# Another order of one turn's pieces on four engines of a two-layer transformer kernel

## The chip, the core and the metric

The kernel runs on one core of a Trainium2 chip. PE is the matrix engine (TensorE), ACT the scalar engine, DVE the vector engine, POOL is GpSimd, SP issues the DMAs. The engines run beside each other and meet through semaphores. The metric is the device time of one execution in microseconds (us).

## The reference, cut to what matters

The input has 32 sequences of 256 tokens with 128 features, all in fp32. Four sublayers follow one another, each with a residual and a layer norm behind it.

```
x = layernorm(x + mala_attn(x))      # a: rotary linear attention, 8 heads, 5-tap conv on v, gate
x = layernorm(x + low_rank_moe(x))   # b: base matmul + one of four low-rank experts (top-1 softmax)
x = layernorm(x + causal_attn(x))    # c: softmax attention in 256 tokens
x = layernorm(x + routed_swiglu(x))  # r, d: grouped top-4 of 16 experts, plus two shared ones
#   g = silu(x @ w1.T); u = x @ w3.T; y = sum_e comb[e] * (g * u)[e] @ w2[e].T + shared
```

## The kernel before, in words

The tokens are cut into 16 blocks of 512 tokens (four tiles of 128). A block goes through five stages, one per turn: **a** (first attention), **b** (low-rank layer and the projections of the second attention), **c** (second attention, and the router **r**), **d** (the experts), **e** (last residual and store). Turn i works on block i in stage a, i-1 in b, i-2 in c, i-3 in d and i-4 in e, so there are 20 turns; in turns 4 to 15 all five stages are there. Six turns are written out ahead (LEAD), ten run in a hardware loop of two turns per pass, and four are written out behind.

Each engine has its own function `turn`, a list of calls in the order in which the engine does them. Nothing is reordered by a scheduler: an engine waits at the first call whose semaphores are not there. The order written in `turn` is therefore the whole plan.

The experts are 9 chunks of 128 hidden units (8 routed, 1 shared). For a chunk c:
- PE `d_hidden(n, odd, c)`: gate part into bank GB and up part into UB. Each is three fp32r matmuls of 512 columns (`mm3`, L331 to L333: high*high, high*low, low*high). For c from 1 to 7 it ends with `d_spread` (L542, a bf16 matmul that spreads the routing weights over 512 columns into CB).
- ACT `d_silu` (L729): silu of GB. DVE `d_gu` (L1041): times UB. DVE `d_hid` (L1051): times CB. Chunk 8 has no routing weight and goes through L1044.
- PE `d_down(n, c)` (L552): the fp32 matmul with w2, accumulated in YB. One such matmul is two records in the trace. `d_down(n, 8)` is the last; ACT `d_y` (L733) copies YB behind it.

GB, UB and CB exist once. So `d_hidden(c+1)` waits for `d_silu(c)` and `d_gu(c)`, and `d_spread(c)` waits for `d_hid(c-1)`.

Pieces of the other stages stand between the chunks. Those the text speaks of, in the order of their data:
- b: `b_small` (PE L443) -> `b_norm`, `b_logits` (DVE L877 to L895, POOL L1183 between) -> `b_exp` (ACT L681) -> `b_first`, `b_weigh` (DVE L900 to L924, the last writes `down_x`) -> `b_dnT` (PE L340 of down_x) -> ACT copy L689 -> `b_up` (PE L455/L456) -> `b_res` and its statistics (DVE L982, L859) -> `ln_of(1)` (POOL L1163, ends with `shift`) -> `b_layer_norm` (ACT L643) -> `c_xT` (PE L340 of x2) -> `c_project`, `c_value` (PE L466, L467, L472).
- r: `r_xT`, ACT `r_hi` (L714, L715), `r_gate` (PE L512), ACT `r_exp` (L719), DVE `r_groups` and `r_combine` (L1006 to L1035, the last writes `comb`), POOL `r_split` (L1138 to L1144), PE `d_cT` of the next turn.
- POOL also has `x3_lo` (L1202), `x2_bias` (L1192), `e_norm` (L1212, L1216) and `c_norm` (L1206, L1208).
- a: `a_kv`, `a_qT_`, `a_den`, `a_num_` (PE L396, L340, L413, L418), `a_rd`, `a_out` (L428); on DVE four `conv_tap` (L933).
- c: `c_pT` (PE L493), ACT L710, `c_av` (PE L499 to L501).

Exp and silu need different function tables on ACT; an ACT_TABLE_LOAD stands where the kind changes.

## Time and profile before

| what | value |
|---|---|
| median of 3 runs | 835.02 us (834.77 to 835.66) |
| span of the profiled execution | 831.0 us |
| PE busy | 759.4 us, 91% |
| DVE busy | 607.2 us, 73% |
| ACT busy | 455.8 us, 55% |
| POOL busy | 416.1 us, 50% |

The page gives the profiled execution's span, from first to last instruction, and no separate time for it; the median of the runs is 4.0 us above the span. Matmul records overlap (the end of one is modelled and lies past the start of the next), so for PE the distance from start to start is what a matmul costs, and not the duration printed in its row.

### The profile page before, as it was taken

The page shows a single profiled execution, that of the slowest core. Times are in us where ns is not written, and L with a number is a line of the kernel's source. Part 1 is how long each engine was busy: PE and PEld are TensorE (multiplying, and loading weights), DVE is VectorE, ACT ScalarE, POOL GpSimd, SP SyncE. Part 2 cuts the span into 40 slices and gives each one's busy share as a digit, 9 for nine tenths or more (in the row PEclk, how much of TensorE's full clock was granted, in tenths as well). Part 3 has the DMA queues.
Part 4 walks back from the last instruction along what each step waited for, and adds up shares of the span by engine and source line. Part 5 has one row for each costly group of instructions (what it writes and reads, how often), then busy time and mean ns, then how long its engine had stood idle before and what let it go on. Part 6 is the DMA issues. An engine that isn't in the chain of part 4 may idle for free.

```text
span 831.0 us, 13767 instructions
## 1 busy us (share of the span) xinstructions
PE 759.4 (91%) x3926; PEld 537.0 (65%) x3926; DVE 607.2 (73%) x1853; ACT 455.8 (55%) x863; POOL 416.1 (50%) x922
## 2 busy tenths in 40 slices
PE   4487689999999999999999999999999999999985
PEld 3375667676767676666767676667767676665552
DVE  2554748878797878778797878788796878785652
ACT  2224266575656666664655666664656666655321
POOL 2425534664646545654636555654636555543322
PEclk9658789999999999999999999999999999999998
DMA  5000000000000000000000000000000000000000
GB/s 222 13 0 14 0 14 1 14 14 13 2 13 14 14 14 13 14 13 13 0 13 13 13 13 13 14 13 13 0 13 13 13 0 13 2 13 0 13 13 13
DMA packets 17526, 13.04 MB, mean 16 GB/s; under 512 B 576, under 2 KB 16960, under 8 KB 17088
## 3 DMA queue, kind: packets, MB, share of 16 engines
q1 hardware_dynamic: 17472, 12.47, 4.7%
q14 instruction: 38, 0.31, 0.1%
q8 instruction: 16, 0.26, 0.1%
HBM read 8.27 MB, written 4.19 MB: 15 GB/s over the span
## 4 chain that ended last, share of the span: by engine, by line
PE 68%; DVE 12%; issue 9%; ACT 5%; POOL 4%; DMA 1%; DVEq 0%; POOLq 0%; SPq 0%; ACTq 0%
PE bank L552 12%; PE bank L340 7%; PE bank L331 6%; PE bank L333 6%; PE bank L332 6%; PE bank L542 4%; PE bank L455 2%; PE bank L428 2%; PE bank L472 2%; PE bank L443 2%; PE bank L413 2%; PE bank L466 2%; PE bank L467 2%; PE bank L371 2%; DVE hid L1051 2%
## 5 line engine op out<-in xcount | busy, mean ns | idle before, releaser
L1041 DVE TENSOR_TENSOR gu<-silu,bank 128x512 f32<-128x512 f32 x128 | 86.5, 676 | 108.3 <-ACT silu L729 72.8
L552 PE MATMUL bank<-hid,whole 128*128 128x512 f32 x288 | 152.9, 614 | 0.3 <-DVE hid L1044 0.3
L331 PE MATMUL bank<-x3T_hi,w_hi 128*128 128x512 f32 x288 | 141.2, 490 | 0.1
L729 ACT ACTIVATE silu<-bank 128x512 f32<-128x512 f32 x144 | 85.8, 596 | 86.8 <-PE bank L333 80.5
L333 PE MATMUL bank<-x3T_hi,w_lo 128*128 128x512 f32 x288 | 113.9, 396 | 0.0
L332 PE MATMUL bank<-x3T_lo,w_hi 128*128 128x512 f32 x288 | 113.7, 395 | 0.0
L1051 DVE TENSOR_TENSOR hid<-gu,bank 128x512 f32<-128x512 f32 x128 | 87.3, 682 | 9.4 <-DVE gu L1041 3.4
L1132 POOL TENSOR_TENSOR qk<-rope_c,rope_s 128x512 f32<-128x512 f32 x32 | 40.6, 1280 | 72.2 <-DVE rope_s L830 72.2
L1163 POOL TENSOR_TENSOR moment<-stats 128x4 f32<-128x4 f32 x192 | 35.9, 219 | 79.1 <-DVE stats L859 78.9
L331 PEld LDWEIGHTS bank<-x3T_hi,w_hi 128*128 128x128 f32 x288 | 54.7, 190 | 21.6 <-issue 10.3
L1163 POOL TENSOR_TENSOR rstd<-moment,whole 128x4 f32<-128x4 f32 x64 | 64.8, 1012 | 5.0
L332 PEld LDWEIGHTS bank<-x3T_lo,w_hi 128*128 128x128 f32 x288 | 54.9, 191 | 16.0 <-issue 10.3
L1150 POOL TENSOR_TENSOR rden_x<-rden,whole 128x512 f32<-128x512 f32 x16 | 17.4, 1088 | 93.1 <-DVE rden L843 93.1
L552 PEld LDWEIGHTS bank<-hid,whole 128*128 128x128 f32 x288 | 46.4, 189 | 25.8 <-DVE hid L1044 13.2
L333 PEld LDWEIGHTS bank<-x3T_hi,w_lo 128*128 128x128 f32 x288 | 54.2, 188 | 12.6
L729 ACT ACT_TABLE_LOAD x45 | 57.7, 1283 | 0.8
L859 DVE BATCH_NORM_STATS2 stats<-res 128x6 f32<-128x128 f32 x256 | 55.8, 281 | 2.2
L542 PE MATMUL bank<-combT,sel_exp_b 48*128 48x512 bf16 x128 | 49.7, 388 | 5.5 <-DVE hid L1051 4.8
L933 DVE SCALAR_TENSOR_TENSOR conv<-vT,whole,conv 128x512 f32<-128x512 f32 x64 | 48.1, 751 | 0.3
L542 PEld LDWEIGHTS bank<-combT,sel_exp_b 48*128 48x128 bf16 x128 | 11.8, 92 | 49.6 <-issue 30.6
L340 PE MATMUL bank<-whole,x 128*128 128x128 f32 x192 | 31.2, 287 | 11.7 <-ACT x L643 8.2
L676 ACT ACTIVATE numT<-bank,v_sum 128x256 f32<-128x256 f32 x32 | 13.4, 470 | 51.8 <-PE bank L418 51.8
(210 smaller groups left out, 1850.7 us busy)
## 6 DMA issues: line engine op xcount, KB each, us to landing
x_in<-x SPq DMA_DIRECT2D x16, 256.0 KB, 3.1
out<-x SPq DMA_DIRECT2D x16, 256.0 KB, 2.3
whole<-w_whole SPq DMA_DIRECT2D x1, 1198.5 KB, 5.6
w_raw<-w SPq DMA_DIRECT2D x1, 1152.0 KB, 9.3
whole<-w_whole SPq DMA_DIRECT2D x1, 1088.0 KB, 11.3
w_raw<-w SPq DMA_DIRECT2D x1, 546.0 KB, 6.9
```

Of the source, the lines that this page charges most:

```text
L331: mm(out, wh, mh, start=True, stop=False)
L332: mm(out, wh, ml, start=False, stop=False)
L333: return mm(out, wl, mh, start=False, stop=True)
L340: last = nc.tensor.transpose(out[0:parts, t * P:(t + 1) * P], src(t), eye)
L542: mm(CB[:], sel_exp_b[:, c * P:(c + 1) * P], combT[:], start=True, stop=True).then_inc(p_C.sem, 1)
L552: mm(YB[:], whole[:, a:a + P], hid[:, c % 2], start=c == 0, stop=c == CHUNKS).then_inc(p_w2.sem, 1)
L729: fn(silu[:, c % 2], GB[:], ACT.Silu).then_inc(a_silu.sem, 1)
L859: nc.vector.bn_stats(stats[k][:, t, :], res[k][:, t, :]).then_inc(v_st[k].sem, 1)
L933: stt(conv[:], vT[:, :, j:j + SEQ], taps[:, j:j + 1], conv[:], ALU.mult, ALU.add).then_inc(v_conv.sem, 1)
L1041: tt(gu[:, c % 2], silu[:, c % 2], UB[:], ALU.mult).then_inc(v_gu.sem, 1)
L1051: tt(hid[:, c % 2], gu[:, c % 2], CB[:], ALU.mult).then_inc(v_hid.sem, 1)
L1163: tt(out, in0, in1, op).then_inc(g_ln[k].sem, 1)
```

## The change

The same calls are made with the same operands; only their order in the four `turn` functions differs. No matmul, activation or vector operation is added or removed, but two ACT table loads per turn fall away, since the exps of b and r now follow one another.

```diff
@@ -560,47 +560,47 @@
                 if d: d_hidden(i - 3, 1 - odd, 0)
                 if d: d_cT(i - 3, live(i - 1))
                 if c: c_scores(i - 2)
+                if a: a_xT_(i, odd, load)
                 if d: d_spread(i - 3, 0)
-                if a: a_xT_(i, odd, load)
                 if e: d_yT(i - 4)
                 if d: d_hidden(i - 3, 1 - odd, 1)
+                if a: a_v_(i)
                 if d: d_down(i - 3, 0)
-                if a: a_v_(i)
                 if d: d_hidden(i - 3, 1 - odd, 2)
                 if c: c_pT(i - 2)
                 if a: a_qk(i)
-                if d: d_down(i - 3, 1)
                 if c: c_av(i - 2)
                 if b: b_xT(i - 1)
+                if d: d_down(i - 3, 1)
+                if a: a_g_(i)
+                if b: b_small(i - 1)
+                if a: a_vT_(i)
                 if d: d_hidden(i - 3, 1 - odd, 3)
-                if b: b_small(i - 1)
-                if a: a_g_(i)
                 if d: d_down(i - 3, 2)
-                if a: a_vT_(i)
                 if d: d_hidden(i - 3, 1 - odd, 4)
+                if a: a_kv(i)
+                if a: a_qT_(i)
                 if d: d_down(i - 3, 3)
-                if a: a_kv(i)
                 if d: d_hidden(i - 3, 1 - odd, 5)
+                if a: a_den(i)
                 if c: r_xT(i - 2, odd)
-                if a: a_qT_(i)
+                if a: a_num_(i)
                 if d: d_down(i - 3, 4)
                 if c: r_gate(i - 2)
                 if b: b_dnT(i - 1)
                 if d: d_hidden(i - 3, 1 - odd, 6)
-                if a: a_den(i)
                 if b: b_up(i - 1)
-                if a: a_num_(i)
                 if d: d_down(i - 3, 5)
+                if a: a_rd(i)
                 if d: d_hidden(i - 3, 1 - odd, 7)
-                if a: a_rd(i)
                 if d: d_down(i - 3, 6)
                 if d: d_hidden(i - 3, 1 - odd, 8)
                 if d: d_down(i - 3, 7)
-                if d: d_down(i - 3, 8)
                 if b: c_xT(i - 1)
                 if a: a_out(i)
                 if b: c_project(i - 1)
                 if b: c_value(i - 1)
+                if d: d_down(i - 3, 8)
 
             for i in range(LEAD):
                 if i == 3:
@@ -740,18 +740,18 @@
                 if d: d_silu(i - 3, 1)
                 if c: c_exp(i - 2)
                 if a: a_v_(i)
+                if c: c_pT(i - 2)
                 if d: d_silu(i - 3, 2)
-                if c: c_pT(i - 2)
                 if b: copy_xT(i - 1, 1, B0)
+                if b: b_small(i - 1)
                 if d: d_silu(i - 3, 3)
-                if b: b_small(i - 1)
                 if a: a_g_(i)
                 if a: a_vT_(i)
                 if d: d_silu(i - 3, 4)
+                if a: a_qT_(i)
+                if d: d_silu(i - 3, 5)
                 if b: b_exp(i - 1)
-                if d: d_silu(i - 3, 5)
                 if c: r_hi(i - 2, odd)
-                if a: a_qT_(i)
                 if c: r_exp(i - 2)
                 if b: b_dnT(i - 1)
                 if d: d_silu(i - 3, 6)
@@ -760,8 +760,8 @@
                 if d: d_silu(i - 3, 8)
                 if b: b_layer_norm(i - 1)
                 if b: copy_xT(i - 1, 2, B0)
+                if b: c_qkv(i - 1)
                 if d: d_y(i - 3)
-                if b: c_qkv(i - 1)
 
             for i in range(LEAD):
                 if i == 1:
@@ -1066,40 +1066,40 @@
                 if d: d_gu(i - 3, 1)
                 if d: d_hid(i - 3, 1)
                 if b: a_layer_norm(i - 1)
+                if a: a_rope(i)
                 if d: d_gu(i - 3, 2)
+                if c: c_res(i - 2)
                 if d: d_hid(i - 3, 2)
-                if a: a_rope(i)
-                if c: c_res(i - 2)
+                if b: b_norm(i - 1, 0)
                 if d: d_gu(i - 3, 3)
-                if b: b_norm(i - 1, 0)
+                if b: b_norm(i - 1, 1)
                 if d: d_hid(i - 3, 3)
-                if b: b_norm(i - 1, 1)
+                if b: b_logits(i - 1)
                 if d: d_gu(i - 3, 4)
-                if b: b_logits(i - 1)
+                if a: a_kv(i)
                 if d: d_hid(i - 3, 4)
-                if a: a_kv(i)
+                if a: conv_tap(i, 1)
                 if b: b_first(i - 1)
-                if b: b_weigh(i - 1)
-                if a: conv_tap(i, 1)
                 if d: d_gu(i - 3, 5)
                 if a: conv_tap(i, 2)
+                if b: b_weigh(i - 1)
                 if d: d_hid(i - 3, 5)
                 if a: conv_tap(i, 3)
                 if c: r_groups(i - 2, 0)
                 if a: conv_tap(i, 4)
                 if c: r_groups(i - 2, 1)
+                if a: a_den(i)
+                if c: r_groups(i - 2, 2)
                 if d: d_gu(i - 3, 6)
-                if c: r_groups(i - 2, 2)
-                if a: a_den(i)
                 if b: b_res(i - 1)
+                if d: d_hid(i - 3, 6)
                 if c: r_groups(i - 2, 3)
-                if d: d_hid(i - 3, 6)
-                if c: r_groups(i - 2, 4)
+                if a: a_att(i)
                 if d: d_gu(i - 3, 7)
                 if d: d_hid(i - 3, 7)
-                if a: a_att(i)
+                if c: r_groups(i - 2, 4)
+                if a: a_gate(i)
                 if d: d_gu(i - 3, 8)
-                if a: a_gate(i)
                 if c: r_combine(i - 2)
                 if a: a_res(i, odd)
 
@@ -1223,13 +1223,13 @@
                 if c: ln_of(2, i - 2)
                 if b: b_norm(i - 1)
                 if c: c_norm(i - 2, odd)
-                if e: e_norm(i - 4)
-                if c: x3_lo(i - 2, odd)
                 if a: a_rd(i)
                 if b: ln_of(1, i - 1)
                 if a: a_mix(i)
+                if b: x2_bias(i - 1)
+                if c: x3_lo(i - 2, odd)
                 if c: r_split(i - 2)
-                if b: x2_bias(i - 1)
+                if e: e_norm(i - 4)
                 if a: ln_of(0, i)
 
             for i in range(LEAD):
```

How the order stands, word for word. In the names, `whole` is the block of constants (w2 and the identity among them), `x_b` is x2 with its bias, a buffer number is left out.

PE, the end of a turn, before:

```order
L333 MATMUL bank<-x3T_hi,w_lo 128x512
L552 MATMUL bank<-hid,whole 128x512 x2
L340 MATMUL bank<-whole,x 128x128 x4
L428 MATMUL bank<-whole,oT 128x128 x4
L466 MATMUL bank<-x2T,w_raw 128x512
L467 MATMUL bank<-x2T,w_raw 128x512
L472 MATMUL bank<-w_raw,x2T 128x128 x4
```

PE, the same place in the change and the first matmul of the next turn:

```order
L333 MATMUL bank<-x3T_hi,w_lo 128x512
L552 MATMUL bank<-hid,whole 128x512
L340 MATMUL bank<-whole,x 128x128 x4
L428 MATMUL bank<-whole,oT 128x128 x4
L466 MATMUL bank<-x2T,w_raw 128x512
L467 MATMUL bank<-x2T,w_raw 128x512
L472 MATMUL bank<-w_raw,x2T 128x128 x4
L552 MATMUL bank<-hid,whole 128x512
L331 MATMUL bank<-x3T_hi,w_hi 128x512
```

The last down-projection (L552) moved from right behind the one before it to the end of the turn, ahead of the next turn's first chunk.

PE, the middle of a turn from the spread of chunk 5 on, before:

```order
L542 MATMUL bank<-combT,sel_exp_b 128x512
L340 MATMUL bank<-whole,x_1 128x128 x4
L340 MATMUL bank<-whole,qk 128x128 x4
L552 MATMUL bank<-hid,whole 128x512
L512 MATMUL bank<-w_raw,x3T 128x16 x4
L340 MATMUL bank<-whole,down_x 96x128 x4
L331 MATMUL bank<-x3T_hi,w_hi 128x512
```

The same place in the change:

```order
L542 MATMUL bank<-combT,sel_exp_b 128x512
L413 MATMUL bank<-ks_m,qT 128x8 x4
L340 MATMUL bank<-whole,x_1 128x128 x4
L418 MATMUL bank<-qT,kv_m 128x256 x2
L552 MATMUL bank<-hid,whole 128x512
L512 MATMUL bank<-w_raw,x3T 128x16 x4
L340 MATMUL bank<-whole,down_x 96x128 x4
L331 MATMUL bank<-x3T_hi,w_hi 128x512
```

`a_den` and `a_num_` (L413, L418) stand ahead of the router's matmul (L512) and of `down_x`; before, they came a chunk later, on both sides of `b_up`.

ACT, the middle of a turn, before:

```order
L729 ACTIVATE silu<-bank 128x512
L681 ACT_TABLE_LOAD
L681 ACTIVATE lg_e<-lg_s 128x16
L729 ACT_TABLE_LOAD
L729 ACTIVATE silu<-bank 128x512
L714 ACTIVATE x3T<-bank 128x512
L715 ACTIVATE x3T_hi<-bank 128x512
L661 ACTIVATE qT<-bank 128x512
L719 ACT_TABLE_LOAD
L719 ACTIVATE ez<-bank 128x64
L689 ACTIVATE downT<-bank 96x512
L729 ACT_TABLE_LOAD
```

The same place in the change:

```order
L729 ACTIVATE silu<-bank 128x512
L661 ACTIVATE qT<-bank 128x512
L729 ACTIVATE silu<-bank 128x512
L681 ACT_TABLE_LOAD
L681 ACTIVATE lg_e<-lg_s 128x16
L714 ACTIVATE x3T<-bank 128x512
L715 ACTIVATE x3T_hi<-bank 128x512
L719 ACTIVATE ez<-bank 128x64
L689 ACTIVATE downT<-bank 96x512
L729 ACT_TABLE_LOAD
```

The exp of b (`lg_e`) moved behind the silu of chunk 5 and next to the exp of r (`ez`), and `qT` ahead of both; two of four table loads are gone.

POOL, the end of a turn, before:

```order
L1155 TENSOR_TENSOR mixT<-attT,conv 128x512
L1186 ISA
L1138 TENSOR_TENSOR comb_b<-comb,whole 128x4x16
L1139 REGISTER_ALU
L1140 TENSOR_TENSOR comb_r<-comb,comb_b 128x64
L1141 REGISTER_ALU
L1142 TENSOR_TENSOR comb_b<-comb_r,whole 128x4x16
L1143 REGISTER_ALU
L1144 TENSOR_TENSOR comb_b<-comb_r,comb_b 128x4x16
L1192 TENSOR_TENSOR x_b<-x,whole 128x512
```

The same place in the change:

```order
L1155 TENSOR_TENSOR mixT<-attT,conv 128x512
L1192 TENSOR_TENSOR x_b<-x,whole 128x512
L1202 TENSOR_TENSOR x3T_lo<-x3T,x3T_hi 128x512
L1186 ISA
L1138 TENSOR_TENSOR comb_b<-comb,whole 128x4x16
L1139 REGISTER_ALU
L1140 TENSOR_TENSOR comb_r<-comb,comb_b 128x64
L1141 REGISTER_ALU
L1142 TENSOR_TENSOR comb_b<-comb_r,whole 128x4x16
L1143 REGISTER_ALU
L1144 TENSOR_TENSOR comb_b<-comb_r,comb_b 128x4x16
L1211 REGISTER_ALU
```

`x_b` and `x3T_lo` stand ahead of the split of `comb`; `x3T_lo` came much earlier in the turn, and so did `centered` and L1216, which now follow the split.

DVE's order: `b_logits` moved ahead of the gu of chunk 4, one conv tap ahead of `b_first` and another ahead of `b_weigh`, and the last part of `r_groups` behind the hid of chunk 7.

## Rows read from the trace of the kernel before

**Rows 1.** The page: the span of the profiled execution.
```profile
span 831.0 us, 13767 instructions
```

**Rows 2.** Timeline, PE, one full turn: start, us, line, operands, count, idle.
```profile
435.66 1.16 PE L472 MATMUL bank<-w_raw,x2T 128*128 128x128 f32 x8
...
455.15 1.02 PE L552 MATMUL bank<-hid,whole 128*128 128x512 f32 x2
456.01 0.60 PE L340 MATMUL bank<-whole,v_one 128*128 128x128 f32 x4
...
460.02 0.48 PE L331 MATMUL bank<-x3T_hi,w_hi 128*128 128x512 f32 x1
...
461.91 0.65 PE L340 MATMUL bank<-whole,x 128*128 128x128 f32 x4
...
462.83 1.02 PE L552 MATMUL bank<-hid,whole 128*128 128x512 f32 x2
464.02 1.07 PE L512 MATMUL bank<-w_raw,x3T 128*128 128x16 f32 x8 [0.17 <-ACT x3T_hi L715]
465.52 0.64 PE L340 MATMUL bank<-whole,down_x 128*96 128x128 f32 x4 [0.43 <-DVE down_x L924]
465.92 0.48 PE L331 MATMUL bank<-x3T_hi,w_hi 128*128 128x512 f32 x1
...
468.36 1.06 PE L413 MATMUL bank<-ks_m,qT 128*128 128x8 f32 x8
469.27 0.47 PE L455 MATMUL bank<-w_raw,x1T 128*128 128x128 f32 x2
...
476.98 2.13 PE L552 MATMUL bank<-hid,whole 128*128 128x512 f32 x4
478.95 0.60 PE L340 MATMUL bank<-whole,x 128*128 128x128 f32 x4
...
482.14 1.16 PE L472 MATMUL bank<-w_raw,x2T 128*128 128x128 f32 x8
```

**Rows 3.** Timeline, PE, a down-projection directly ahead of an fp32r group.
```profile
470.50 0.31 PE L456 MATMUL bank<-up_x,downT 96*128 96x128 f32 x1
...
471.56 1.02 PE L552 MATMUL bank<-hid,whole 128*128 128x512 f32 x2
...
472.65 0.40 PE L332 MATMUL bank<-x3T_lo,w_hi 128*128 128x512 f32 x1
```

**Rows 4.** Timeline, DVE: down_x in turn 1, then in a full turn.
```profile
55.77 0.22 DVE L924 TENSOR_TENSOR down_x<-down_m,down_x 128x60 f32<-128x60 f32 x1
...
464.30 1.16 DVE L924 TENSOR_TENSOR down_x<-down_m,down_x 128x60 f32<-128x60 f32 x1
```

**Rows 5.** Timeline, POOL, the same full turn and the end of the one before.
```profile
435.84 0.30 POOL L1138 TENSOR_TENSOR comb_b<-comb,whole 128x64 bf16<-128x64 f32 x1 [3.82 <-DVE comb L1035]
...
437.24 1.29 POOL L1192 TENSOR_TENSOR x_b<-x,whole 128x512 f32<-128x512 f32 x1
...
464.11 1.27 POOL L1202 TENSOR_TENSOR x3T_lo<-x3T,x3T_hi 128x512 fp32r<-128x512 f32 x1 [1.10 <-ACT x3T_hi L715]
...
475.73 0.20 POOL L1163 TENSOR_TENSOR shift<-mean,rstd 128x4 f32<-128x4 f32 x1
```

**Rows 6.** Timeline, ACT, the layer norm of b.
```profile
476.98 1.64 ACT L643 ACTIVATE x<-res,shift,rstd 128x128 f32<-128x128 f32 x4
```

**Rows 7.** Timeline, DVE, the last operations of the router in that turn.
```profile
479.59 0.23 DVE L1013 TENSOR_TENSOR above<-masked,top 128x64 f32<-128x64 f32 x1
...
482.02 0.22 DVE L1035 TENSOR_TENSOR comb<-wsel,winv 128x64 f32<-128x64 f32 x1
```

**Rows 8.** Timeline, turn 16, all engines: around the matmul that waits for probT.
```profile
724.30 1.28 ACT L729 ACT_TABLE_LOAD   x1
...
727.01 0.49 PE L499 MATMUL bank<-cv,probT 128*128 128x128 f32 x2 [0.95 <-ACT probT L710]
```

**Rows 9.** Waits: engine line <- cause, us in total, times, longest.
```profile
DVE gu L1041 <- issue: 10.3, 4, 2.8
```

## The prediction

> **What bounds the kernel now.** I read the timeline of PE first, because PE's order is what the change rewrites most. From one value projection to the next a full turn lasts 482.14 - 435.66 = 46.48 us [rows 2]. Twelve of the twenty turns are full, so a tenth of a microsecond in the turn is worth 1.2 us in the program, and nearly all of the 831.0 us span [rows 1] is such turns. Inside one, PE goes from piece to piece without idling except where a start-to-start distance is larger than the same piece has elsewhere. The reader is to look for those places [rows 2]:
>
> - A down-projection costs 456.01 - 455.15 = 0.86. The one ahead of the router's L512 takes 464.02 - 462.83 = 1.19: PE waits 0.33 for the copy of x3T.
> - Eight short fp32 records cost 469.27 - 468.36 = 0.91. L512 to down_x takes 465.52 - 464.02 = 1.50: PE waits 0.59 for DVE's down_x.
> - A chunk with its spread costs 461.91 - 460.02 = 1.89. The one behind down_x takes 468.36 - 465.92 = 2.44: 0.55 of wait, first for the gu and then for the hid of chunk 5, which stand on DVE behind down_x.
> - The last two down-projections take 478.95 - 476.98 = 1.97 where 1.72 is their price: 0.25 for the shared chunk's product on DVE.
>
> Together 1.72 us of waits per turn that an order can remove. The rest is PE's own work, which the change keeps.
>
> **The change part by part.**
>
> The pairing of down-projections with fp32r groups I cost at nothing. A pair is there already: L552 at 471.56 is followed by L331, whose successor L332 starts at 472.65 [rows 3]. That is 1.09, the 0.86 of a down-projection and 0.23 for one fp32r matmul, with nothing saved or lost against 0.86 where transposes follow [rows 2]. What changes a little is what follows a spread; four spreads get a longer follower. I put that at +0.15 per turn. Two restarts behind short pieces fall away (`a_g_` behind `b_small`, `b_up` behind `a_den`), which gives about as much back. Both stay inside the range.
>
> The middle of the turn. `a_den` and `a_num_` now stand ahead of `r_gate` and `b_dnT`. They put 0.91 (L413) [rows 2] and about 0.9 (L418, from 470.50 to 471.56 less one L456) [rows 3] between the copies and PE's need of them. On ACT the exp of b moves behind the silu of chunk 5, which makes it later by about one silu and one chunk, but it shares its table load with the exp of r. A load is 1.28 [rows 8], and two of them go. On DVE, `b_weigh` gets one conv tap more ahead of it, yet POOL no longer runs a long operation beside it. down_x takes 0.22 in turn 1, where POOL is idle, and 1.16 in a full turn, where it starts at 464.30 and ends at 465.46 just after x3T_lo of POOL (464.11 to 465.38) ends [rows 4, 5]. With x3T_lo at the end of the turn that 0.94 goes. Laying the pieces out by these prices, down_x is ready about 0.6 before PE reaches it, and the hid of each of chunks 2 to 6 about 0.5 to 0.7 before its spread. So I take the first three waits, 1.47, as gone. The bounds are 1.47 and, if each of those five slacks is overestimated, some 0.5 less.
>
> The end of the turn. `d_down(8)` leaves the place where it waited (0.25 gone) and goes behind `c_value`, where its operand is long ready. But it was cover. The chain `b_up`, residual, statistics, POOL's layer norm, ACT's layer norm, `c_xT` does not get shorter. From the last L456 (470.50) the `shift` of POOL comes 5.43 later (475.93) [rows 3, 5], the norm on ACT takes 1.64 [rows 6], and with a small delay by the silu of chunk 8 the transposes of x2 can start 7.2 to 7.6 behind that L456. PE needed 478.95 - 470.50 = 8.45 for the work between, so nothing waited. Of this work `a_num_` (0.91), `d_down(8)` (0.86) and the wait of 0.25 leave: 6.43 stays. So a **new wait of 0.75 to 1.15 at `c_xT`** appears; I take 0.9. This is where half of the gain goes, and no other engine's slack helps, since each link of the chain waits for the one before.
>
> The router's tail. POOL now does x_b and x3T_lo (1.29 and 1.27) [rows 5] right behind ACT's norm, and DVE computes `comb` in that stretch. From `above` (479.59) to the end of `comb` (482.24) it takes 2.65 with POOL idle, as the idle 3.82 ahead of L1138 tells [rows 5, 7]. Most of these operations read two SBUF tensors, as down_x does. If they are held as down_x was, the first is through only when x3T_lo ends, and `comb` comes some 1.4 later. Counted from the value projection: the last L456 at 34.84 - 1.47 + 0.86 + 0.91, about 35.1; the norm ends at 42.4, x3T_lo at 44.9, `comb` at 47.5, the split (437.24 - 435.84 = 1.40 [rows 5]) at 48.9. PE wants it for `d_cT` behind 1.16 of projection, 0.86 of down-projection and chunk 0 in the next turn, at about 49.0. So the wait there is 0 to 0.4; I take 0.15.
>
> The row on down_x shows one operation held to the end of one POOL operation. [...] No row of before has `comb` beside a long POOL operation. [...]
>
> `d_y` on ACT moves behind `c_qkv`; the silu of chunk 0 waits for a PE that is 0.86 later anyway. `e_norm` on POOL now delays the layer norm of stage a by some 2, which DVE needs only 3 or more later. Both cost nothing.
>
> Sum for a full turn: -1.72 + 0.9 + 0.15 = -0.67. Turn 3 is nearly full; thirteen turns give -8.7.
>
> The ends of the program. In turn 16 PE idles 0.95 at L499 for probT, whose copies stand on ACT behind a table load of 1.28 and a silu [rows 8]; the change puts them ahead. Turn 17 has the same place. With some of turn 16's other waits I take -1.9 (bounds 0 and -4). In turns 1 and 2 there are no experts, and the chain of b sets the pace. Two conv taps now stand ahead of `b_weigh`, and `a_den` and `a_num_` ahead of `b_up`: about +1.6 in turn 1 and -0.5 in turn 2 (bounds 0 and +3). Sum: -8.7 - 1.9 + 1.1 = -9.5. The span becomes 821.5, and with the 4.0 that lie outside it the median 825.5.
>
> **The rivals.**
>
> 1. *The new wait at `c_xT` isn't there*, because statistics and norm run faster or earlier than the distances above say. Then the turn gains 1.5 or more and the time is 835.0 - 13 x 1.55 - 0.8 = 814, with part of it 811 to 819. Against it: the chain of 5.43 and 1.64 has the same links in the same order.
> 2. *Most of the gain stays in the middle.* The slacks of 0.5 to 0.7 are sums over a dozen operations on two engines. If they are gone, PE waits 0.1 to 0.3 at several spreads and at down_x, and whatever delays `b_up` delays the turn in full. At 0.5 of such waits the time is 835.0 - 13 x 0.17 - 0.8, about 832; at 0.65 it is within the noise.
> 3. *Slower: `b_up` comes late.* Mechanism: the exp of b behind the silu of chunk 5, then `b_weigh` behind two conv taps, down_x, `b_dnT`, copy, `b_up`. Everything behind `b_up` is a chain now, so each further microsecond is paid in every turn. It decides at the point where down_x ends 1.3 later than I lay it out (0.6 of slack and 0.67 of gain). At 2.0 later the turn loses 0.7 and the time is 844. For it: the silu of chunk 2 is now held by `c_pT` and its table load, which starts DVE's work late in the turn. Against it: down_x gets 0.94 shorter, and PE has 1.8 more to do before it.
> 4. [...] DVE stood still four times, 10.3 in sum, at the first gu of a pass of the loop, for nothing that the profile shows [rows 9]; ACT shows no such row. ACT's last operation ahead of the branch is now `d_y`. Would ACT stand still as long, silu 0 and combT would be 2.6 late, and `a_xT_` would wait about 1.1 in four turns: 825.5 + 4.4, about 830. [...]
>
> **How the numbers follow.** My forecast, 820 to 830.5: 0.50. Rival 1 (811 to 820): 0.10. Rivals 2 and 4 together, 830.5 to 833.3: 0.15, and the part of rival 2 that is within 0.2% (833.3 to 836.7): 0.13. Rival 3 (836.7 to 848): 0.12. A measurement of this kernel tells about 0.2% from no change. So faster 0.75, same 0.13, slower 0.12. The range from 818 to 836 leaves out most of rival 1 and all of rival 3, about 2 in 10.
>
> **What would show it.** PE's turn at 45.8 instead of 46.48; no idle at L512, at down_x or at the spread behind it; down_x at 0.22; idle of about 0.9 ahead of the transposes of x2, released by ACT L643; `comb` stretched past 3.5 from the first `above`, with a single operation that ends with a POOL operation; L499 without its 0.95. The forecast is wrong if the transposes of x2 don't wait (rival 1), if down_x or a spread waits (2), or if the last L456 stands later than 36 behind the value projection (3).

## The result: slower, 846.3 us where 825.5 was forecast

| what | before | after |
|---|---|---|
| median of the runs side by side | 834.89 us (828.18 to 835.66, 4 runs) | 846.34 us (845.92 to 847.25, 4 runs) |
| ratio | 1 | 1.0169 (1.0129 to 1.0208) |
| span of the profiled execution | 831.0 us | 845.5 us |

The kernel before takes anything from 828.2 to 836.6 over the runs of this case, so experiments are told as a ratio to runs of before on the same chip, or, closer, by the length of a turn in the trace: from one value projection (L472) to the next, as in the prediction.

Where the 14.5 us between the two spans are: up to turn 3 the change is 1.5 ahead (L472 at 155.64, before 157.14). Turns 4 and 5 take 45.83 and 45.85, near the 45.80 of the forecast, and are another 1.0 ahead (before takes 46.33 and 46.32 there). The ten turns from 6 to 15 take 46.9 or 48.5 where before took 46.47: 14.5 behind. The rest of the program loses 2.5.

Four names are needed. `g_tie` and `g_beat` are two small operations in part 4 of `r_groups` on DVE. `mixT` is what POOL writes in `a_mix`. The gate is DVE's `a_gate`, which reads mixT and writes `oT` for PE's `a_out` (L428).

Turn 5 first, the last of the turns that are written out. DVE, POOL and PE at its end, from the timeline of the changed kernel (start, us, engine, line, operands, count, idle ahead and what ended it):

```profile
241.64 0.26 DVE L967 SCALAR_TENSOR_TENSOR g_tie<-g_diff,whole 128x64 f32<-128x64 f32 x1
241.94 1.20 DVE L970 SCALAR_TENSOR_TENSOR g_beat<-g_diff,g_tie 128x64 f32<-128x64 f32 x1
...
243.78 0.69 DVE L853 TENSOR_TENSOR oT<-mixT,gT 128x512 f32<-128x512 f32 x1
```
```profile
241.78 1.28 POOL L1155 TENSOR_TENSOR mixT<-attT,conv 128x512 f32<-128x512 f32 x1
244.00 1.60 POOL L1192 TENSOR_TENSOR x_b<-x,whole 128x512 f32<-128x512 f32 x1 [0.94 <-ACT x L643]
```
```profile
243.98 0.66 PE L340 MATMUL bank<-whole,x 128*128 128x128 f32 x4 [0.66 <-ACT x L643]
244.52 1.16 PE L428 MATMUL bank<-whole,oT 128*128 128x128 f32 x8
```

The same place in turn 9, in the hardware loop:

```profile
431.80 1.34 DVE L967 SCALAR_TENSOR_TENSOR g_tie<-g_diff,whole 128x64 f32<-128x64 f32 x1
433.17 0.23 DVE L970 SCALAR_TENSOR_TENSOR g_beat<-g_diff,g_tie 128x64 f32<-128x64 f32 x1
...
434.04 1.77 DVE L853 TENSOR_TENSOR oT<-mixT,gT 128x512 f32<-128x512 f32 x1
```
```profile
431.78 1.28 POOL L1155 TENSOR_TENSOR mixT<-attT,conv 128x512 f32<-128x512 f32 x1
433.99 1.27 POOL L1192 TENSOR_TENSOR x_b<-x,whole 128x512 f32<-128x512 f32 x1 [0.94 <-ACT x L643]
```
```profile
432.29 1.02 PE L552 MATMUL bank<-hid,whole 128*128 128x512 f32 x2
433.97 0.66 PE L340 MATMUL bank<-whole,x 128*128 128x128 f32 x4 [0.66 <-ACT x L643]
435.86 1.16 PE L428 MATMUL bank<-whole,oT 128*128 128x128 f32 x8 [1.24 <-DVE oT L853]
...
438.66 1.16 PE L472 MATMUL bank<-w_raw,x2T 128*128 128x128 f32 x8
```

Read them as two ties. `g_tie` has two operands in SBUF. In turn 5 it starts 0.14 ahead of POOL's mixT and takes 0.26; the next operation, g_beat, is then held until mixT ends (1.20 instead of 0.23, to 243.14, where mixT ends at 243.06). In turn 9 it starts 0.02 behind mixT and is itself held, 1.34, and g_beat's 0.23 comes on top. So the gate (oT, two SBUF operands again) starts 0.72 or 0.98 behind the end of mixT. POOL's x_b starts 0.94 behind that end. In turn 5 the gate is 0.22 ahead of x_b and takes 0.69; in turn 9 it is 0.05 behind and takes 1.77, past the end of x_b. `a_out` (L428) waits for it. In all ten turns of the loop g_tie starts 0.02 or 0.03 behind mixT and takes 1.34, and the gate starts 0.03 to 0.05 behind x_b and takes 1.77 or 1.78.

The group of all sixteen gates, before and then after (duration min/median/max in ns):

```profile
L853 DVE TENSOR_TENSOR oT<-mixT,gT x16: 691/693/693, 30.1 to 710.9; 128x512 f32<-128x512 f32 x16
```
```profile
L853 DVE TENSOR_TENSOR oT<-mixT,gT x16: 684/1769/1776, 30.3 to 720.2; 128x512 f32<-128x512 f32 x16
```

The second part of the loss stands in PE's own rows of every second turn. Turn 8, and the stretches 387 to 390 and 390 to 393 with their granted clock (column PEclk, third from the end); the same stretch of turn 9 (436 to 439) stands at 1.00:

```profile
387.32 1.91 PE L428 MATMUL bank<-whole,oT 128*128 128x128 f32 x8 [1.24 <-DVE oT L853]
389.02 1.92 PE L466 MATMUL bank<-x2T,w_raw 128*128 128x512 f32 x2
```
```profile
387.00:390.00 3.00, 2.68 (x10) 2.16 (x11) 2.81 (x15) 0.00 (x0) 1.40 (x1) 0.59 0.00 0
390.00:393.00 3.00, 3.00 (x13) 1.71 (x12) 2.26 (x9) 1.47 (x3) 1.78 (x5) 0.84 0.00 0
...
436.00:439.00 3.00, 3.00 (x15) 1.77 (x16) 2.74 (x16) 0.91 (x2) 0.94 (x1) 1.00 0.00 0
```

The 0.59 is the mean of a stretch in which the clock changes: microsecond by microsecond the same view gives 0.77 from 387 on, 0.50 from 388 to 390, 0.53 from 390 on and 1.00 from 391 on. The text calls this 0.50 the half clock. Under it L428 takes 1.91 instead of 1.16, L466 1.92 instead of 1.02. It costs 1.6 in each of turns 6, 8, 10, 12, 14 and 15. What PE did before it is the idle of 0.66 and of 1.24; the other turns of the loop have the same two idles and a granted clock of 1.00.

So the loop loses 1.08 to the late gate (46.93 against 45.85) in ten turns, 10.8, and 1.6 to the half clock in six, 9.6: together 20.4. The span came out 24.0 above its forecast (845.5 against 821.5); what is left of that, 3.6, lies in the main in the last turns. The median missed by 20.8 and not by 24.0, because the forecast added 4.0 to the span where the runs show less.

The forecast's other marks are there. The middle of the turn has no idle at L512, at down_x or behind it (where [rows 2] had 0.17 and 0.43), and down_x takes 0.22 (1.16 in [rows 4]):

```profile
422.32 0.96 PE L512 MATMUL bank<-w_raw,x3T 128*128 128x16 f32 x8
423.13 0.62 PE L340 MATMUL bank<-whole,down_x 128*96 128x128 f32 x4
423.50 0.48 PE L331 MATMUL bank<-x3T_hi,w_hi 128*128 128x512 f32 x1
```
```profile
422.30 0.22 DVE L924 TENSOR_TENSOR down_x<-down_m,down_x 128x60 f32<-128x60 f32 x1
```

The last L456 stands 34.9 behind the value projection, where the forecast had 35.1.

### The profile page after: what moved, and what is told of

Read it like the earlier page. It is cut to its first block and busy times, and to the rows that moved or that the text cites. A ratio compares the mean times of both kernels' runs of the same rounds, so it can differ in the third digit from the quotient of the medians.

```text
span 845.5 us, 13739 instructions
## 1 busy us (share of the span) xinstructions
PE 759.3 (90%) x3926; PEld 539.1 (64%) x3926; DVE 627.5 (74%) x1853; ACT 422.8 (50%) x835; POOL 418.5 (50%) x922
## 5 line engine op out<-in xcount | busy, mean ns | idle before, releaser
L331 PE MATMUL bank<-x3T_hi,w_hi 128*128 128x512 f32 x288 | 153.0, 531 | 1.3 <-DVE gu L1041 1.3
L552 PE MATMUL bank<-hid,whole 128*128 128x512 f32 x288 | 153.2, 614 | 0.1
L332 PE MATMUL bank<-x3T_lo,w_hi 128*128 128x512 f32 x288 | 113.9, 396 | 0.0
L331 PEld LDWEIGHTS bank<-x3T_hi,w_hi 128*128 128x128 f32 x288 | 54.8, 190 | 28.9 <-issue 20.4
L332 PEld LDWEIGHTS bank<-x3T_lo,w_hi 128*128 128x128 f32 x288 | 54.8, 190 | 26.7 <-issue 20.2
L828 DVE TENSOR_TENSOR rope_c<-bank,whole 128x512 f32<-128x512 f32 x32 | 22.0, 687 | 45.3 <-PE bank L384 45.3
L552 PEld LDWEIGHTS bank<-hid,whole 128*128 128x128 f32 x288 | 45.8, 191 | 13.6 <-issue 9.7
L340 PE MATMUL bank<-whole,x 128*128 128x128 f32 x192 | 32.0, 292 | 20.8 <-ACT x L643 20.8
L933 DVE SCALAR_TENSOR_TENSOR conv<-vT,whole,conv 128x512 f32<-128x512 f32 x64 | 47.7, 746 | 0.1
L340 PEld LDWEIGHTS bank<-whole,x 128*128 128x128 f32 x192 | 23.2, 152 | 33.6 <-ACT x L643 33.1
```

Of the source, the lines that this page charges most:

```text
L331: mm(out, wh, mh, start=True, stop=False)
L332: mm(out, wh, ml, start=False, stop=False)
L340: last = nc.tensor.transpose(out[0:parts, t * P:(t + 1) * P], src(t), eye)
L552: mm(YB[:], whole[:, a:a + P], hid[:, c % 2], start=c == 0, stop=c == CHUNKS).then_inc(p_w2.sem, 1)
L933: stt(conv[:], vT[:, :, j:j + SEQ], taps[:, j:j + 1], conv[:], ALU.mult, ALU.add).then_inc(v_conv.sem, 1)
```

## The experiments

Theory A is the lock, read from the rows above: a DVE operation with two operands in SBUF that starts behind a POOL operation is held by it (g_tie 1.34 instead of 0.26, the gate 1.77 instead of 0.69), and a POOL operation by a gate ahead of it (x_b 1.60 instead of 1.27); the changed order puts two pairs of them within 0.1 of each other, and the half clock is a consequence. The rivals stand with each expectation. Every kernel was timed beside the kernel before.

### Take the tie away: part 4 of r_groups back

```diff
+                if c: r_groups(i - 2, 4)
                 if a: a_att(i)
                 if d: d_gu(i - 3, 7)
                 if d: d_hid(i - 3, 7)
-                if c: r_groups(i - 2, 4)
                 if a: a_gate(i)
```

> The last part of r_groups goes back ahead of the gu of chunk 7 on DVE, nothing else. Theory A (the gate is held): in the changed kernel oT starts at 434.04, 0.05 behind the start of x_b on POOL (433.99), is held until x_b ends and takes 1.77 instead of 0.69, and L428 waits for it; it starts that late because g_tie was itself held beside mixT (1.34 instead of 0.23) and 0.9 of r_groups follows. With r_groups early, oT starts when mixT ends (433.06), 0.9 ahead of x_b, takes 0.69, and L428 doesn't wait. Every full turn is then like turns 4 and 5 of the changed kernel, 45.9, and the clock stays at full speed: about 828 us (825 to 832). Theory B (only the place of r_groups on DVE matters, no lock): oT comes 1.6 to 1.9 earlier too and the time is the same 828. Theory C (the loss is the wait at c_xT, whose pause lets the clock fall): the wait of 0.9 stays, so every second turn stays at 48.4 and the time is about 845.

821.89 us (821.14 to 825.30), 0.9853 (0.9814 to 0.9893) of before. The gate starts 0.82 ahead of x_b and takes 0.69; turns are 45.67 and none of the loop is at half clock (granted clock 1.00 from 190 to 720 us), so Theory C is out. It is 6 below the expected 828; the turn, 45.67 for 45.9, accounts for about half of that. Theories A and B forecast the same here; e2 and e3 tell them apart. The whole change with this one line elsewhere has the lowest median of the case (e11, at 822.25, is the same within the noise). The wait at `c_xT` is not seen in it, because PE now waits for the gu of chunk 7 just before it:

```profile
425.52 0.50 PE L331 MATMUL bank<-x3T_hi,w_hi 128*128 128x512 f32 x1 [0.59 <-DVE gu L1041]
...
427.36 0.60 PE L340 MATMUL bank<-whole,x 128*128 128x128 f32 x4
```

### The gate ahead of part 4

```diff
+                if a: a_gate(i)
                 if c: r_groups(i - 2, 4)
-                if a: a_gate(i)
                 if d: d_gu(i - 3, 8)
```

> The gate goes ahead of the last part of r_groups on DVE, nothing else; r_groups keeps its late place. Theory A: oT starts at the end of mixT, 0.9 ahead of x_b, takes 0.69, L428 doesn't wait; turns of 45.9, about 828 us (825 to 833); comb comes up to 1.3 later than in the change, since masked is then late and above runs beside x_b and x3T_lo, so d_cT may wait some 0.2 to 0.5. Theory B (DVE has too much to do at that place): gu of chunk 8 and comb move back by the 1.6 of r_groups, the gain is at most half: 835 to 840. Theory C: 845.

850.96 us, 1.0212 (1.0169 to 1.0254), 23 above what was expected. The gate is indeed free (0.69) and L428 waits no more, but part 4 now runs beside x_b and x3T_lo, and both g_tie and g_beat are held:

```profile
436.69 1.18 DVE L967 SCALAR_TENSOR_TENSOR g_tie<-g_diff,whole 128x64 f32<-128x64 f32 x1
437.91 1.19 DVE L970 SCALAR_TENSOR_TENSOR g_beat<-g_diff,g_tie 128x64 f32<-128x64 f32 x1
```
```profile
445.16 0.42 PE L340 MATMUL bank<-ident_b,comb_b 128*96 128x128 bf16 x4 [2.00 <-POOL comb_b L1144]
```

The first runs beside x_b (436.52 to 437.79), the second beside x3T_lo (437.75 to 439.01). `comb` comes 2.0 too late for `d_cT`. The expectation had the wait there at a few tenths, with the moved work at its free duration, which is the error of the prediction made again: the lock didn't vanish with the shift, it took the next pair (1.18 and 1.19 where the two run free at 0.22 to 0.26).

### Take only the gate's second SBUF operand away

```diff
-                tt(oT[:], mixT[:], gT[:], ALU.mult).then_inc(v_oT.sem, 1)
+                tt(oT[:], mixT[:], A0[:], ALU.mult).then_inc(v_oT.sem, 1)
```

> The order is that of the change, but the gate multiplies mixT by the PSUM bank A0 in place of gT in SBUF, so it has one SBUF input (this leaves the gate's values out; A0 holds the old numerator). Theory A: oT starts where it starts now, 0.05 behind x_b, but isn't held: 0.69 instead of 1.77, L428 waits 0.2 instead of 1.24, no slow clock in the tail; turns of 46.0 to 46.2, about 830 us (827 to 834). Theory B: the operand's place doesn't matter, 1.77 stays, 846 us.

823.79 us, 0.9868 (0.9822 to 0.9915), some 3 below the expected range. This kernel leaves the gate's values out of its result. g_tie is held as in the change (1.34), the gate starts 0.04 behind x_b as in the change, and still takes 0.68:

```profile
426.47 0.68 DVE L853 TENSOR_TENSOR oT<-mixT,bank 128x512 f32<-128x512 f32 x1
```
```profile
426.43 1.27 POOL L1192 TENSOR_TENSOR x_b<-x,whole 128x512 f32<-128x512 f32 x1 [0.94 <-ACT x L643]
```

So it isn't the moment nor the load of DVE, but the operands. Turns are 45.85, with a granted clock of 1.00 from 190 to 720 us. It also shows that the hold of g_tie costs nothing that shows in the turn by itself: it only puts the gate where x_b holds it. The rows of the gate in turns 5 and 9 of the change show that the one that starts first holds the other, in both directions: x_b itself takes 1.60 when the gate is 0.22 ahead and 1.27 when it is behind. In turn 5 of this kernel the gate is 0.21 ahead too, with its operand in PSUM, and x_b takes 1.28.

### Take x_b away from there

```diff
                 if a: a_mix(i)
-                if b: x2_bias(i - 1)
-                if c: x3_lo(i - 2, odd)
                 if c: r_split(i - 2)
+                if b: x2_bias(i - 1)
```

(x3_lo stands behind c_norm again, as before.)

> On POOL x3_lo goes back behind c_norm and x2_bias back behind r_split; e_norm stays behind them, DVE, ACT and PE as in the change. Theory A: oT still starts at about 434.0, but no long POOL operation runs there: 0.69, L428 waits 0.2 at most; comb takes 2.65 from the first above instead of up to 5; down_x may be held again by x3T_lo (up to 1.2, of which 0.6 is slack). Turns of 45.9 to 46.4, about 831 us (827 to 835). Theory B (r_groups late on DVE): 844 to 847.

831.64 us, 0.9972 (0.9949 to 0.9994); turns 46.42. The gate is free, and the wait at down_x is back, as expected. But down_x itself is held only in the turns written out (1.17) and takes 0.22 in the loop. There it is the operation ahead of it, a cast with one operand in SBUF, that x3T_lo holds (1.32, and 0.22 in every turn of the change):

```profile
417.46 1.32 DVE L922 CAST down_x<-down_m 128x120 fp32r<-128x120 f32 x1
418.81 0.22 DVE L924 TENSOR_TENSOR down_x<-down_m,down_x 128x60 f32<-128x60 f32 x1
```
```profile
417.44 1.26 POOL L1202 TENSOR_TENSOR x3T_lo<-x3T,x3T_hi 128x512 fp32r<-128x512 f32 x1 [5.12 <-ACT x3T_hi L715]
```

### More work on POOL

```diff
+                for k in range(3):
+                    tt(nudge[:, k], const("neg_half"), const("half"), ALU.add)
                 tt(mixT[:], attT[:], conv[:].rearrange("p s l -> p (s l)"), ALU.add).then_inc(g_mix.sem, 1)
```

> The change with three tiny additions more on POOL in every turn (each 128x4, about 0.2 us, into a scratch tile that nobody reads), right ahead of mixT. So it does strictly more work, and mixT comes about 0.5 later. Theory A (a start of 20 ns decides: g_tie of DVE, two SBUF inputs, starts just behind mixT of POOL in the changed kernel and is held to its end, and with it the gate, which then starts just behind x_b and is held again): with mixT 0.5 later g_tie and g_beat run at 0.23 to 0.26 ahead of it, only the last short operation of the fourth part of r_groups is held to mixT's end, and the gate starts some 0.3 ahead of x_b and takes 0.69. L428 waits no more, or under 0.45; the turn is 45.8 to 46.0 all the way, with no turn at half clock; time 825 to 829. Rival B (the gate is late because DVE simply has too much to do there, or because POOL's row is too full): more work on POOL cannot help; turns of 46.9 and 48.5 as in the change, 845 to 850.

824.18 us (821.36 to 825.58), 0.9911 (0.9882 to 0.9940), just below the expected range, turns 45.76 and 45.85. Three needless operations in every turn make the changed kernel some 22 us faster. (The lines of this kernel lie 1 to 3 further on.)

```profile
422.80 0.27 DVE L968 SCALAR_TENSOR_TENSOR g_tie<-g_diff,whole 128x64 f32<-128x64 f32 x1
423.10 0.26 DVE L971 SCALAR_TENSOR_TENSOR g_beat<-g_diff,g_tie 128x64 f32<-128x64 f32 x1
423.39 0.22 DVE L973 TENSOR_REDUCE g_rank<-g_beat 128x16 f32<-128x64 f32 x1
423.64 0.89 DVE L975 TENSOR_SCALAR penalty<-g_rank 128x16 f32<-128x16 f32 x1
...
424.70 0.68 DVE L854 TENSOR_TENSOR oT<-mixT,gT 128x512 f32<-128x512 f32 x1
```
```profile
422.79 0.49 POOL L1157 TENSOR_TENSOR nudge<-whole 128x4 f32<-128x4 f32 x3
423.23 1.27 POOL L1158 TENSOR_TENSOR mixT<-attT,conv 128x512 f32<-128x512 f32 x1
424.99 1.53 POOL L1195 TENSOR_TENSOR x_b<-x,whole 128x512 f32<-128x512 f32 x1 [0.49 <-ACT x L644]
```

mixT starts 0.43 later against `shift` than in the change, g_tie and g_beat both start ahead of it and run free, and the gate is 0.29 ahead of x_b. Only `penalty`, small and with one operand, is held to the end of mixT (0.89 instead of 0.17, to 424.53, where mixT ends at 424.50).

### Why from turn 6 on

Turns 6 to 15 are the hardware loop. The same kernel with twelve turns written out ahead of it:

```diff
-    LEAD = 6
+    LEAD = 12
```

> The changed kernel with the same order in every turn, only that twelve turns are written out ahead of the hardware loop instead of six, and the loop makes two passes instead of five. Theory A (the order itself is on an edge: g_tie starts 0.13 ahead of mixT in the turns written out and 0.02 behind it in those of the loop, and only that decides whether g_tie and the gate are held): turns 4 to 11 take 45.8 to 46.0, g_tie 0.26 in them, and from turn 12 on it goes back to 46.9 and 48.5. Six turns are saved 1.8 each: 834 to 838. Rival B (after the first turns something else builds up, whatever the loop): the gate is held from turn 6 on as in the change, 845 to 848.

832.78 us, 1.0006 (0.9979 to 1.0033), just below the expected range, and the change of pace stands exactly where the loop now begins: turns 4 to 11 take 45.93 to 45.96, turns 12 to 15 take 47.27, 48.57, 46.83 and 48.56. The gate in turn 11 and in turn 12:

```profile
516.44 0.68 DVE L853 TENSOR_TENSOR oT<-mixT,gT 128x512 f32<-128x512 f32 x1
...
562.64 1.77 DVE L853 TENSOR_TENSOR oT<-mixT,gT 128x512 f32<-128x512 f32 x1
```

In turn 11 g_tie starts 0.24 ahead of mixT, in turn 12 0.01 behind it. What in the loop moves the two engines by 0.15 to 0.25 against each other wasn't looked for.

### An earlier norm makes it slower

Two edits in DVE's row (part 4 ahead of the gu of chunk 7, attT behind it), and then on top of them the norm of b ahead of the silu of chunk 8 on ACT:

```diff
                 if c: r_groups(i - 2, 3)
+                if c: r_groups(i - 2, 4)
+                if d: d_gu(i - 3, 7)
                 if a: a_att(i)
-                if d: d_gu(i - 3, 7)
                 if d: d_hid(i - 3, 7)
-                if c: r_groups(i - 2, 4)
```
```diff
-                if d: d_silu(i - 3, 8)
                 if b: b_layer_norm(i - 1)
+                if d: d_silu(i - 3, 8)
```

> Against the change: on DVE the fourth part of r_groups stands ahead of the gu of chunk 7, and attT behind that gu (in e1_groups_early both, the groups and attT, stood ahead of it, and PE waited 0.86 for this gu in chunk 8). Theory A (the chain from the last b_up over residual, statistics, POOL's norm and ACT's norm to c_xT sets the turn, and the 0.86 in e1 only stood in the place of the wait at c_xT): the wait in chunk 8 falls to 0 to 0.3 and one of 0.5 to 0.9 comes back at c_xT; the turn stays at 45.6 to 45.9, time 820 to 825. Rival B (the late gu of chunk 7 was a cost of its own): the turn falls to about 44.9 and the time to 811 to 814.

> Against e6_gu7_first: on ACT b_layer_norm stands ahead of the silu of chunk 8 (d_down(8) stays at the end of the turn, so nobody needs that silu soon). Theory A (the chain to c_xT sets the turn): the four norm activations start when POOL's shift ends and not behind the silu, 0.4 to 0.5 earlier, and the turn is shorter by as much, 45.2 to 45.4; time 815 to 819; comb not more than 0.3 later. Rival B (the chain doesn't set the turn): no difference from e6_gu7_first.

The first takes 825.70 us, 0.9938 (0.9908 to 0.9967), turns 45.87 and 45.96. The turn's length is Theory A's, the place of the waits isn't: not at `c_xT`, but 0.3 at chunk 8, 0.4 at d_down(7) for the hid of chunk 7, and 0.3 at comb_b. The second takes 835.77 us, 1.0043 (1.0016 to 1.0069), turns 46.68, where Theory A had expected 45.2 to 45.4 and Rival B the 45.9 of e6. The norm does come earlier, and with it x_b, which now starts as soon as mixT is done, 0.07 ahead of the gate:

```profile
432.02 1.74 DVE L853 TENSOR_TENSOR oT<-mixT,gT 128x512 f32<-128x512 f32 x1 [0.87 <-POOL mixT L1155]
```
```profile
431.95 1.27 POOL L1192 TENSOR_TENSOR x_b<-x,whole 128x512 f32<-128x512 f32 x1
```
```profile
433.82 1.16 PE L428 MATMUL bank<-whole,oT 128*128 128x128 f32 x8 [1.05 <-DVE oT L853]
```

A norm that came earlier lost 0.8 a turn, by the same tie.

### The cover that d_down(8) was

```diff
                 if d: d_down(i - 3, 7)
+                if d: d_down(i - 3, 8)
                 if b: c_xT(i - 1)
                 if a: a_out(i)
                 if b: c_project(i - 1)
                 if b: c_value(i - 1)
-                if d: d_down(i - 3, 8)
```

(On top of e6; `d_y` and the gu of chunk 8 stand where they stood before.)

> Against e6_gu7_first: d_down(8) goes back to its place of before, behind d_down(7) and ahead of c_xT (with d_y on ACT ahead of c_qkv, and the gu of chunk 8 ahead of the gate on DVE, as before). Theory A (the wait at c_xT is what d_down(8) used to cover): no wait at c_xT, 0.2 to 0.4 at d_down(8) for the shared product, the turn is 45.1 to 45.4, time 814 to 818. Rival B (moving d_down(8) is neutral, the wait at c_xT has another cause): turn within 0.15 of e6_gu7_first. Rival C (the 0.86 which PE gains is lost at d_cT, since comb comes no earlier): idle of 0.3 or more at the transposes of comb_b, turn 45.4 or more.

825.14 us, 0.9921 (0.9892 to 0.9951), turns 45.87 and 45.96: nothing gained over e6. That is Rival B's turn, and Rival C fits as well, with an idle of 0.34 at the transposes of comb_b. The run couldn't answer its question, since e6 has no wait at `c_xT` for a cover to fill. The clean test needs a kernel that has the wait, which is e5:

```diff
                 if d: d_down(i - 3, 7)
+                if d: mm(CB[:], whole[:, w2:w2 + P], hid[:, 1], start=True, stop=True)
                 if b: c_xT(i - 1)
```

> Against e5_pool_extra, in which only the wait of 0.88 at c_xT is left at the end of the turn: one fp32 matmul of 512 columns more on PE (w2 of chunk 0 times the product of chunk 7, into the bank CB, read by nobody), right behind d_down(7) and ahead of c_xT, where d_down(8) stood before the change. It is 0.86 of additional PE work in each full turn. Theory A (the wait at c_xT is ended by a chain that doesn't pass through PE, and is as long as the cover that was moved away): the wait at c_xT falls to 0 to 0.1, and turn and time stay as in e5, 45.7 to 45.9 and 821 to 826. Rival B (PE is the bound there, the idle only stands where PE waits anyway for other reasons): the turn grows by 0.86 to 46.65, time 835.

824.07 us, 0.9910 (0.9882 to 0.9939), turns 45.77 to 45.95, against 824.18 for e5. 0.86 more of PE work in every turn with experts costs nothing:

```profile
425.31 1.02 PE L556 MATMUL bank<-hid,whole 128*128 128x512 f32 x2
426.16 0.61 PE L341 MATMUL bank<-whole,x 128*128 128x128 f32 x4
```

### What the half clock needs

> The changed kernel with the one additional fp32 matmul of e9 (w2 of chunk 0 times the product of chunk 7, into CB, read by nobody) behind d_down(7): 0.86 of PE work that fills the idle of 0.66 ahead of the transposes of x2, and leaves the idle of 1.24 ahead of L428 as it is, since the gate doesn't depend on PE. Theory A (PE's clock falls to half behind the two idles together; by the trace every second turn of the changed kernel spends 1.6 at half clock, while kernels with one of the two idles alone don't): L428 still waits 1.4 to 1.5 in each turn of the loop, the gate still takes 1.77, but no turn of the loop is at half clock; turns of 46.9 to 47.0 throughout and 836 to 840, so 6 to 10 less with more work. Rival B (the idle at L428 alone, or the loop's parity, makes the half clock): 46.9 and 48.5 in turn as in the change, 845 to 848.

The same matmul in the changed kernel gives 836.77 us, 1.0050 (1.0022 to 1.0078), turns of 46.94 to 46.98 from turn 7 on (turn 6 takes 47.28). The lock is as in the change, L428 waits its 1.24, but the granted clock stays at 1.00:

```profile
385.99 1.16 PE L428 MATMUL bank<-whole,oT 128*128 128x128 f32 x8 [1.24 <-DVE oT L857]
386.98 1.02 PE L466 MATMUL bank<-x2T,w_raw 128*128 128x512 f32 x2
```
```profile
387.00:390.00 3.00, 3.00 (x15) 1.75 (x14) 2.73 (x13) 1.40 (x3) 0.36 (x2) 1.00 0.00 0
```

So in the changed kernel the half clock goes when the first of the two idles is filled: more work there saves 9.6. In no turn of the loop does it stand behind the idle at L428 alone (here, and in e8 with 1.05), or behind the one at `c_xT` alone (e3, e5): the granted clock of all four is 1.00 from 190 to 720 us. The two together aren't sufficient, since they leave turns 7, 9, 11 and 13 at full clock, and they aren't the only pattern: e2 has an idle of 0.65 at `c_xT` and one of 1.9 to 2.0 at comb_b 8.7 later in the turns of its loop, and its turn 12 alone falls to a granted clock of 0.59 behind them and takes 49.35 where the others take 47.6 to 47.7. What decides it from turn to turn is open.

### POOL's order alone, and one attempt at a better kernel

```diff
                 if c: c_norm(i - 2, odd)
-                if e: e_norm(i - 4)
-                if c: x3_lo(i - 2, odd)
...
                 if a: a_mix(i)
+                if b: x2_bias(i - 1)
+                if c: x3_lo(i - 2, odd)
                 if c: r_split(i - 2)
-                if b: x2_bias(i - 1)
+                if e: e_norm(i - 4)
```

> The kernel before with POOL's new order alone (x_b and x3T_lo ahead of the split of comb, centered and x4 behind it). Theory A (the lock): down_x takes 0.22 as x3T_lo no longer runs beside it, so the 0.6 at down_x and part of the 0.55 behind it go; but x_b and x3T_lo then run beside DVE's comb, hold one or two of its operations, and comb is some 1.0 to 1.4 later while PE wants it 0.9 earlier. A wait of 0.5 to 1.0 appears at the transposes of comb_b, and the turn is 46.1 to 46.6, time 830 to 837. Rival B (comb has slack): turn 45.4 to 45.7, time 821 to 825.

827.38 us, 0.9947 (0.9918 to 0.9977), turns 46.20 and 46.30: the turn is Theory A's, the time lies below its range. down_x is free (0.22), and most of that is given back at comb_b:

```profile
434.72 0.42 PE L340 MATMUL bank<-ident_b,comb_b 128*96 128x128 bf16 x4 [0.80 <-POOL comb_b L1144]
```

From start to start this wait is 0.96. In turns 4 and 5 of the changed kernel it is 0.20 and 0.31, and in its loop there is none. Which of the other moves makes the difference wasn't tried.

The last one puts part 3 of r_groups and gscore ahead of the gu of chunk 6, the norm ahead of silu 8, and the gu of chunk 8 between r_combine's maxima and the rest, all on top of e1:

> Against e1_groups_early: on DVE the third part of r_groups and gscore stand ahead of the gu of chunk 6, where DVE idled 0.70, on ACT the norm of b ahead of the silu of chunk 8, and on DVE the gu of chunk 8 between the four maxima and the rest of r_combine. Theory A (the gate now starts well ahead of x_b, and the chain to c_xT and the gu of chunk 7 bind at nearly the same time): the wait in chunk 8 falls from 0.86 to 0.3 to 0.5, the norm on ACT starts 0.4 earlier, the turn is 45.2 to 45.4 and the time 815 to 819. Rival B (DVE's row from the last b_up on is what binds, and reordering in it only moves the wait): 45.6 or more, 821 and up, with the wait at chunk 8, d_down(7) or comb_b.

822.25 us, 0.9885 (0.9835 to 0.9935), turns 45.73 to 45.85: Rival B. The moved operation met POOL's rden_x (417.85 to 418.98) and was held, 1.06 instead of the 0.17 it takes in the change:

```profile
417.95 1.06 DVE L959 TENSOR_TENSOR cross<-pair_hi 128x16 f32<-128x16 f32 x1
```

## Why the prediction was wrong, step by step

- **No cost for pairing, +0.15 for the followers of a spread.** The first is right: down(3) ahead of an fp32r group costs in the change what it cost in [rows 3], 417.00 - 416.54 to the first L331 and 0.63 from there to L332, 1.09 together. The second is of the right kind: down(6), which follows a spread, costs 429.93 to 431.13, 1.20, so 0.11 more; the others weren't measured one by one.
- **The middle, -1.47.** Right: all three waits are gone, and down_x takes 0.22. Its reason was half the truth: e4 shows that the same operation of POOL can also hold the cast ahead of down_x (1.32 instead of 0.22).
- **d_down(8) as cover, a new wait of 0.75 to 1.15 at `c_xT`, 0.9 taken.** Right: 0.82 by the start-to-start distance (433.97 - 432.29, less the 0.86 of a down-projection; 0.66 is shown as idle, released by ACT L643). e9 shows what it is: 0.86 more of PE's work there fills it and costs nothing.
- **`comb` held once, 0.15 at `d_cT`.** The author's estimate, carried over to `comb` from the 1.16 of down_x alone. Right in turns 4 and 5: one operation starts when x_b ends (245.60) and is held to the end of x3T_lo (245.56 to 246.82), and the wait is 0.20 and 0.31, from start-to-start distances:

```profile
245.60 1.30 DVE L1014 TENSOR_TENSOR equal<-masked,top 128x64 f32<-128x64 f32 x1
```

In the loop, where the gate is late, nothing of `comb` is held (2.68 from `above` to its end in turn 9) and this wait is gone. So L428 waits 1.35 longer than in turn 5, from start to start, and the turn grows by 1.08 only.

- **Sum per turn -0.67.** It was measured where the tie is absent: turns of the loop take 45.76 and 45.85 in e5, against 45.80 forecast. Turns 4 and 5 of the change take 45.83 and 45.85, but before was at 46.3 there, so they gained 0.5 each and not 0.67.
- **The step that failed** is the one that isn't there. In the part on "the router's tail" the prediction applied the lock to down_x and to `comb`, and to no other operation. The change moves part 4 of r_groups behind the hid of chunk 7, where it runs beside mixT, and x_b to the place where the gate starts. Neither new pair was priced. POOL's and DVE's rows should have been laid side by side for every operation between chunk 7 and the projections. The two pairs started 0.02 and 0.05 on the wrong side; 0.14 and 0.22 on the other, in turn 5, g_tie and the gate were free (0.26 and 0.69). The prediction put them at nothing; the runs showed an idle of 1.24 at L428 and 1.08 a turn in ten turns, 10.8. Only the gate's hold is paid for: with g_tie held but the gate not (e3) the turn is 45.85. What in the hardware loop brings the two engines to the tie is open.
- **The half clock**, 9.6 of the miss, stood nowhere. The forecast knew of a new idle at `c_xT` and not of a second one close behind it, nor that a granted clock of 0.50 would stand behind the two in every other turn. Whether it could have been foreseen is open, since no run tells what decides it.
- **The ends.** Turns 1 and 2 were forecast at +1.1; up to turn 3 the change gained 1.5 in its profiled execution. That gain isn't shown to be the order's. e12 has the same first turns and reaches the same L472 at 152.44 instead of 155.64: its turn 2 takes 38.2 where the change's takes 40.85, and from 90 to 110 us its granted clock is 0.75 and the change's 0.51 (0.62 in before). Turns 16 and 17 were forecast at -1.9. Turn 16 gained 0.8 (41.51 against 42.28), and what follows it lost 3.3. The wait at L499 shrank from 0.95 [rows 8] to 0.63 instead of going, in both turns, and each has a new one behind it. They aren't the whole loss, since e5 has the same waits and takes 74.65 from there to the end, where the change takes 77.52 and before 74.24:

```profile
750.33 0.50 PE L331 MATMUL bank<-x3T_hi,w_hi 128*128 128x512 f32 x1 [1.33 <-DVE gu L1041]
...
785.60 0.39 PE L542 MATMUL bank<-combT,sel_exp_b 48*128 48x512 bf16 x1 [1.52 <-DVE hid L1051]
```

- **The 4.0 us outside the span** were too much: the profiled execution of the change took 847.25 against a span of 845.5, and its other runs show 1.8 as well. The median of before and its profiled execution are different executions.
- **Rivals.** None occurred. Rival 3 was on the right side with 844, but the transposes of x2 wait for the norm as forecast, and down_x isn't late. Rival 4: ACT's waits in the change have no row released by issue, while DVE's gu has one again (9.4 in four). The slower result was put at 0.12, for another mechanism.

## What to carry to other kernels

When an order moves a DVE operation with two SBUF operands or a POOL operation, lay the two engines' rows side by side over the whole stretch and price every pair that can overlap: here the one that started second was held until the first ended, for up to 1.1 us (g_tie 1.34 instead of 0.26, the gate 1.77 instead of 0.69). A margin of a few hundredths is no margin: 0.02 and 0.05 decided here. If a reordered kernel changes its pace between turns with the same instructions, look for an operation whose duration has two values (here the gate, 0.69 and 1.77). Where PE has two idles close together, look at the granted clock behind them: filling one of them, 0.66 a turn, took 9.6 us off ten turns of the loop here, more than its length.

## What the runs showed of the hardware

- The hold isn't confined to operations with two SBUF operands: a CAST with one took 1.32 instead of 0.22 (e4), a TENSOR_SCALAR of 128x16 0.89 instead of 0.17 (e5). A TENSOR_REDUCE beside the same mixT took its usual 0.22, and the gate with one operand in PSUM 0.68 beside x_b (e3).
- A start 0.02 behind the other's is enough to be held for its whole length: g_tie took 1.34 beside the 1.28 of mixT, and 0.26 where it started 0.14 ahead.
- The granted clock was 0.50 for some 3 us, 0.59 over the stretch from 387 to 390, behind idles of PE of 0.66 and 1.24 in six turns of ten (and once in e2, behind 0.65 and 2.01), and stayed at 1.00 behind 1.24 alone (e13) or 1.05 alone (e8).
- A needless 0.86 of matmuls in each turn made the changed kernel 9.6 us faster (e13), and a needless 0.49 of POOL's additions in each turn some 22 us (e5).
